# A two-branch layer on eight cores: the next block's quantising moved from slice 4 to slice 0 of a feed-forward block, the previous block's transposes and down projection one slice later, and a third residual buffer

## The reference

```python
xn = _layernorm(x, axis=-1)
x = x + _L0_attn_ref(xn, Wq, Wk, Wv, Wf, g_w, Wo) + _L0_ffn_ref(xn, w_gate, w_up, w_down)
```

```python
def _act_quant(x):
    scale = 127.0 / clip(max(abs(x), axis=-1, keepdims=True), 1e-05)
    return clip(round(x * scale), -128.0, 127.0) / scale
def _bitlinear(x, w):
    return einsum('bsi,oi->bso', _act_quant(x), _weight_quant(w))
gate = silu(_bitlinear(xn, w_gate))          # 1024 -> 4096
up = _bitlinear(xn, w_up)                    # 1024 -> 4096
return _bitlinear(gate * up, w_down)         # 4096 -> 1024
```

## Time and profile before

| | |
|---|---|
| time, median of 3 runs | 1782.69 us (1772.68 to 1785.46) |
| time of the profiled execution | 1769.45 us |
| its span on the slowest core | 1767.9 us |
| spans of the eight cores | 1743.3 to 1767.9 us |
| granted TensorE clock, mean by core | 0.909 to 0.921 |
| busy share of the span: PE, DVE, ACT, POOL | 81%, 59%, 32%, 19% |

### The profile page before, as it was taken

How to read it: one execution, slowest core, us unless ns; L and a number is a source line. 1 busy time by engine, 2 the same in 40 slices (tenths; PEclk the granted TensorE clock), 3 DMA queues, 4 the chain that set the end, 5 groups by cost and what they waited for, 6 DMA issues and landing times.

```text
span 1767.9 us, 25430 instructions; the slowest of 8 cores (1743.3 to 1767.9 us)
## 1 busy us (share of the span) xinstructions
PE 1438.2 (81%) x8500; PEld 765.3 (43%) x8500; DVE 1046.1 (59%) x1663; ACT 557.0 (32%) x986; POOL 338.1 (19%) x317
## 2 busy tenths in 40 slices
PE   4778989866678776666667799999999999999998
PEld 1333545544355444444444344444444444444443
DVE  3455455687755577778887345555555544455553
ACT  2563224433466744443434211111111111111111
POOL 1000001333334333333334011111111100111110
PEclk9888999887799888887888899999999999999999
DMA  9997987154555555544452911011111111011110
GB/s 164 221 202 194 237 252 219 55 141 144 153 164 178 169 155 152 151 149 159 148 161 72 316 42 42 25 42 36 42 42 42 42 42 35 33 42 42 39 29 18
DMA packets 126112, 202.99 MB, mean 115 GB/s; under 512 B 58272, under 2 KB 78752, under 8 KB 124832
## 3 DMA queue, kind: packets, MB, share of 16 engines
q1 hardware_dynamic: 120080, 180.39, 35.2%
q0 software_dynamic: 5904, 20.97, 5.3%
HBM read 167.78 MB, written 29.36 MB: 112 GB/s over the span
## 4 chain that ended last, share of the span: by engine, by line
PE 50%; DVE 18%; DMA 16%; issue 9%; ACT 4%; SPq 2%; POOL 1%; DVEq 1%; ACTq 0%; POOLq 0%
PE ps L266 47%; DMA stg<-wdT 4%; DMA stg<-wgT 4%; DVE stI L290 3%; PE ps L271 3%; DMA gu_s<-stB 2%; DMA xin<-xp 2%; DMA stg<-wuT 2%; DVE q L290 2%; DVE stB L457 1%; DMA wf<-wfT 1%; DVE b_st L300 1%; DVE b_w L300 1%; DMA xin<-xr 1%; DVE S2f L300 1%
## 5 line engine op out<-in xcount | busy, mean ns | idle before, releaser
L266 PE MATMUL ps<-wgu,xnTb 128*128 128x512 fp8e4 x2048 | 464.4, 386 | 7.0 <-DMA xnTb<-xnb 6.5
L266 PEld LDWEIGHTS ps<-wgu,xnTb 128*128 128x128 bf16 x2048 | 201.5, 100 | 252.7 <-issue 29.3
L283 ACT ACTIVATE sg<-ps,ccol 128x512 f32<-128x512 f32 x128 | 87.7, 685 | 512.7 <-PE ps L266 476.7
L266 PE MATMUL ps<-wd,qT 128*128 128x512 fp8e4 x1024 | 224.0, 379 | 0.0
L286 DVE TENSOR_TENSOR gu<-ps,sg 128x512 f32<-128x512 f32 x128 | 88.3, 690 | 154.0 <-PE ps L266 137.1
L286 POOL TENSOR_TENSOR xa<-xa,xin 128x1024 f32<-128x1024 f32 x16 | 38.0, 2374 | 618.3 <-DMA xa<-at_s 618.3
L266 PEld LDWEIGHTS ps<-wd,qT 128*128 128x128 bf16 x1024 | 100.2, 98 | 120.9 <-issue 0.5
L300 DVE SCALAR_TENSOR_TENSOR ob<-ps,ccol,xa 128x512 f32<-128x512 f32 x32 | 24.0, 751 | 185.4 <-PE ps L266 185.4
L420 DVE TENSOR_REDUCE part<-stg 128x1 f32<-128x1024 f32 x64 | 77.7, 1219 | 60.9 <-DMA stg<-wgT 30.3
L304 POOL CAST S1b<-S1f 128x512 bf16<-128x512 f32 x64 | 44.4, 693 | 352.7 <-DVE rinv L905 154.3
L457 DVE TENSOR_SCALAR stB<-stI 128x1024 fp8e4<-128x1024 int8 x96 | 87.0, 907 | 35.6 <-DMA gu_s<-stB 19.7
(11 more groups left out here) (146 smaller groups left out, 2330.9 us busy)
## 6 DMA issues: line engine op xcount, KB each, us to landing
stg<-wgT SPq DMA_DIRECT2D x64, 512.0 KB, 5.5
stg<-wuT SPq DMA_DIRECT2D x64, 512.0 KB, 5.2
stg<-wdT SPq DMA_DIRECT2D x64, 512.0 KB, 4.9
xin<-xr SPq DMA_DIRECT2D x32, 512.0 KB, 4.8
xin<-xp SPq DMA_DIRECT2D x16, 512.0 KB, 6.1
gu_s<-stB SPq DMA_DIRECT2D x64, 128.0 KB, 3.1
at_s<-b_wo SPq DMA_DIRECT2D x32, 256.0 KB, 2.0
wgu<-gu_s POOLq DMA_DIRECT2D x8, 1024.0 KB, 19.5
```

Of the source, the lines that this page charges most:

```text
L266: return pe(lambda e: e.matmul(out=out, lhsT=lhsT, rhs=rhs, start=start, stop=stop, skip_group_check=True), *toks, mark=mark)
L283: return sc(lambda e: e.activation(out=out, in_=in_, func=func, **kw), *toks)
```

## The change

In the loop over blocks, `prep_x(b + 1)` and `prep_xa(b + 1)` go from behind slice 4 to behind slice 0 of turn `b`. The transposes of quarters 0 and 1 go behind slice 1 and those of quarters 2 and 3 behind slice 2. The down projection goes behind slice 3. Within slice 0, the next block's preparation is written behind `gu_el(b, 0)`.

Since the next block's residual is now loaded before the down projection of the previous block has read its own, `xa` has three buffers instead of two, with a semaphore of its own for the third load. For the same reason the scale columns `ccol` get their dependencies split: columns 0 to 3 of a block wait for the quantising that reads them (`("col", s)`), and column 13, which the down projection reads, has its own (`("dcl", s)`).

```diff
         for n in (["x0", "x1", "t0", "t1", "st0", "st1", "st2", "qs0", "qs1",
-                   "a0", "a1", "o0", "o1", "o2", "o3", "y0", "y1", "wd", "gw"]
+                   "a0", "a1", "o0", "o1", "o2", "o3", "y0", "y1", "y2", "wd", "gw"]
...
-        xa = [at("xa%d" % i, 1024, F32, S0 + 4096 + i * 4096) for i in range(2)]
-        ob = [at("ob%d" % i, 512, F32, S0 + 12288 + i * 2048) for i in range(4)]
+        xa = [at("xa%d" % i, 1024, F32, S0 + 4096 + i * 4096) for i in range(3)]
+        ob = [at("ob%d" % i, 512, F32, S0 + 16384 + i * 2048) for i in range(4)]
...
-            ta = dma("y%d" % s, sp, xa[s], d_at[b * 128:(b + 1) * 128, :],
-                     B[b]["a0"], B[b]["a1"], upd_end, V.get(("xa", s)))
-            d["xa"] = tt(gp, xa[s], xa[s], xin[s], ALU.add, d["tx"], ta)
+            a = b % 3
+            ta = dma("y%d" % a, sp, xa[a], d_at[b * 128:(b + 1) * 128, :],
+                     B[b]["a0"], B[b]["a1"], upd_end, V.get(("xa", a)))
+            d["xa"] = tt(gp, xa[a], xa[a], xin[s], ALU.add, d["tx"], ta)
...
             d["ds"] = ts(dv, ccol[:, k + 13:k + 14], m, wsc[:, 2:3], ALU.mult, wsc_t[2],
-                         s2=1.0 / 127.0, op1=ALU.mult)
+                         V.get(("dcl", s)), s2=1.0 / 127.0, op1=ALU.mult)
...
             V["gu"] = []
+            V[("col", s)] = V["gu"]
...
                 t = stt(ob[o], bk[half].ap, ccol[:, s * 20 + 13:s * 20 + 14],
-                        xa[s][:, hsl(half)], ALU.mult, ALU.add, p, d["ds"], d["xa"],
+                        xa[b % 3][:, hsl(half)], ALU.mult, ALU.add, p, d["ds"], d["xa"],
...
-            V[("xa", s)] = t
-            V[("col", s)] = t
+            V[("xa", b % 3)] = t
+            V[("dcl", s)] = t
...
                 if b < NO:
                     gu_pe(b, sl)
                     gu_el(b, sl)
-                if sl in (0, 1):
-                    t_part(b - 1, 2 * sl)
-                    t_part(b - 1, 2 * sl + 1)
-                if sl == 2:
-                    down(b - 1)
-                if sl == 4 and b + 1 < NO:
+                if sl == 0 and b + 1 < NO:
                     prep_x(b + 1)
                     prep_xa(b + 1)
+                if sl in (1, 2):
+                    t_part(b - 1, 2 * sl - 2)
+                    t_part(b - 1, 2 * sl - 1)
+                if sl == 3:
+                    down(b - 1)
             if b < NO:
                 gu_quant(b)
```

## The result

| | before | changed |
|---|---|---|
| time, median of 4 runs | 1784.08 us | 1824.82 us |
| ratio, 95% interval | | **1.0166 (1.0124 to 1.0207)** |
| time of the profiled execution | 1769.45 us | 1800.83 us |
| its span on the slowest core | 1767.9 us | 1799.3 us |
| turns 1 to 14 of the loop | 670.5 us, 47.9 each | 708.6 us, 50.6 each |

The change made the kernel slower, by about 30 us. In two of the changed kernel's four runs, and in one of before's, the cores of one die ran at a lower clock, which puts the changed kernel's median high; the ratio leaves such runs out, and the changed kernel's other two took 1800.83 and 1807.02 us. The forecast was 1815 us, within 1783 to 1828, and against the profiled execution 1801 us.

The account below looks back on a forecast made before the run. PE was taken to bound the loop. Turns with a preparation become 43.2 + 5.0 + 2.3 = 50.5 us; +37 over turns 1 to 14 and -5 in turn 15 give +32, so 1782.7 + 32 = 1815 us, range 1783 to 1828.

Parts of the forecast that it names:

- The floor of a turn: PE's least time for one loop turn at full clock: eight slices, down projection and transposes, 43.2 us.
- Both old waits go: PE's waits in turns 1 to 14 for `qb` and for the next block's input `xnTb` were to vanish.
- The new wait: PE, after slice 2, was to wait 5.0 us for the bank that DVE's first copy of transposed quarters empties.
- The walk on DVE: DVE's instructions in order, with undisturbed durations: preparation ends t = 14.0, first copy t = 15.4, PE's third transposes t = 16.3.
- The clock: PE was to run at half clock behind the new wait, through transposes and most of slice 3, losing 2.3 us.
- its bounds of 3.1 and 1.75: Clock losses in us read behind two shorter PE waits in the kernel before, bounding the 2.3 us loss.
- almost all half clock: Claim about the remaining 1.6 us of a turn before, beyond PE's 43.2 us minimum and 3.1 us of waits.
- The sum: Turns 1 to 14 lose 36.5 to 37.5 us, turn 15 gains 5.1 us, together +32 us.
- The collision booked at nothing: POOL's add no longer delays DVE's quantising, 2.0 us shorter a turn; no separate gain counted.
- The absolute time: +32 us gave 1801 us on the profiled execution; put on the median, 1782.7 + 32 = 1815 us.
- The rivals: Clock stays up or wait is shorter, within 1%: 0.20; nothing replaces the waits: 0.06; half clock lasts longer: 0.14.
- nothing would take the waits' place: Rival: DVE has the first copy done when PE arrives; turns of 43.2 us, 4% faster; chance of over 1% gain 0.06.

Follow-up runs that it names:

- e1: Changed kernel with the next block's preparation moved to slice 1, behind the copies of the first two transposed quarters; ratio 0.9592, turns of 43.23 us.
- e3: Changed kernel with the preparation moved to slice 3, between the transposes and the down projection; ratio 0.9601, turns of 43.23 us.
- e8: e1 with two residual buffers instead of three, the residual's load and POOL's add written behind the down projection; ratio 0.9582, turns of 43.23 us.
- e2: Changed kernel with the preparation moved to slice 1 but ahead of the transposes and their copies; turns of 50.48 us, no ratio formed.
- e7: Changed kernel with the minimum over the rows computed three times, making the preparation 2.6 us longer; ratio 1.036, turns of 52.94 us.
- e10: Changed kernel with only the maximum and minimum left in slice 0, the rest of the preparation moved to slice 3; ratio 0.9731, turns of 45.14 us.
- e4: Changed kernel with 20 useless matmuls a turn on PE between slice 2 and the transposes of quarters 2 and 3; ratio 1.0018, turns of 48.49 us.
- e9: Kernel before, with only the row load and the residual's load and POOL add moved behind slice 2's down projection; ratio 0.9783, turns of 45.86 us.
- e5: Kernel before, with only the transposes and down projection one slice later, preparation left behind slice 4; ratio 0.9712, turns of 45.11 us.
- e6: Kernel before, with only the preparation moved to slice 0 and three residual buffers, transposes and down projection not moved later; ratio 1.0257, turns of 51.50 us.

## Why the prediction was right

- **The floor of a turn, 43.2 us.** Turn 15 of the changed kernel and all turns of e1, e3 and e8 are 43.23 us.
- **Both old waits go.** No wait for `xnTb` or `qb` in turns 1 to 14. In turn 2 the first two quarters of `qb` were there by t = 6.1, and PE came at t = 6.9.
- **The new wait.** The walk on DVE put the first copy at t = 15.4 and the transposes at 16.3; turn 2 has 15.3 and 16.15. The wait was 4.87 us for 5.0 forecast, at the place and for the engine named. e2 excludes gate and up's banks as its cause, and e7 and e10 tie it to the DVE time ahead of the copies.
- **The clock.** Forecast 2.3 us a turn from the 4.99 us wait of the last turn; measured 50.61 less 43.23 less 4.85, or 2.5 us, of which e4 took 2.1 away. That 2.3 met it is in part luck. The prediction read the earlier trace rows against transposes of 0.89 us, but the first 16 take 1.52 us at full clock, as they wait for POOL's quarter. Read against that, the clock cost some 1.7 us in the last turn, and 2.5 and 1.1 us where the prediction has its bounds of 3.1 and 1.75. For the same reason the 1.6 us that a turn of before has beyond floor and waits is not "almost all half clock": its slow rows come to some 0.9 us a turn, an estimate by the same reading of its rows. The forecast also took the loss as the same in each turn, but turns range from 49.4 to 51.3 us at nearly equal waits.
- **The sum.** Turns 1 to 14 came to +38.1 us for +37, turn 15 to -5.1 as forecast. Together that is +33; the profiled spans differ by 31.4 us. The mixer, which the change leaves alone, makes up the difference: turn 1 starts at 1020.74 us against 1022.3.
- **The collision booked at nothing.** The change takes it away: the quantising took 3.52 us, and the add ran at t = 19.65 for 20 forecast. That this needs no term of its own holds because the walk on DVE started from the undisturbed turn. Its gain sits in the 5.0 us: with the 2 us still ahead of the copies the wait would be some 2 us longer, by e7's slope (an estimate, not run). In before it was on the path, as e9 shows; in e5, which has it and no preparation ahead of the copies, PE no longer waits for ACT's `qb`.
- **The absolute time.** I put the change on the median of the runs shown, 13 us above the profiled execution. The two runs of the changed kernel that the ratio uses lie at 1801 and 1807 us, nearer to the sum on the profiled execution; the stated 1815 was high by this choice and not by a step of the argument.
- **The rivals.** The clock fell in every turn with a preparation, and the wait had its full length. That nothing would take the waits' place failed in this order, and is what e1 does: it forecast 4% faster, and moving the preparation past two copies gives 4.1%.

What stays open is what decides the clock's share in a single turn. The turns of the changed kernel differ by up to 1.9 us at waits that differ by 0.4 us. Nor does the length of a wait decide whether the clock falls: slice 1 ran at full clock behind a wait of 2.04 us in before, as shown above, and at 0.67 behind one of 1.53 us in e9. No run here changed only that.

## What to carry to other kernels

Moving work earlier on an in-order engine is judged by what it is moved ahead of: ask for each item behind it who waits for it, and put the work behind the last copy or eviction that the bounding engine needs, ahead of a stretch in which the engine itself waits. Two waits that a change removes are worth their length only if nothing else ends at the same place; walk the next wait with the durations of the trace. On TensorE price a wait with the slow rows behind it, and look whether a cheap edit elsewhere, here moving an add on POOL, takes part of the wait away without a reorder.

## What the runs showed of the hardware that was not expected

- Useless matmuls in a wait paid for themselves: the same PE order with 20 of them in the 4.9 us gap ran 2.1 us a turn faster (e4), clock 1.00 for 0.94.
- A wait of 1.53 us, with one of 0.46 us behind it, was followed by a slice at a granted clock of 0.67 in e9, while slice 3 ran at full clock behind each of e10's waits of 1.47 to 1.82 us.
- The half clock's cost depends on where it falls: 1.7 us lost in slice 1 of e6 made the wait behind it 1.7 us shorter, and the turn no longer.
- Its size does not follow the wait: beyond its wait a turn costs 2.53 us at 4.85 us of wait and 2.24 us at 7.47 us (e7).
